# One step less between a node block's first products and its feed-forward part, in a fused GNN layer on one core

## The chip, the core and the metric

The kernel is one program on one core of one Trainium2 chip. Five engines run side by side, each through its own list of instructions in order: TensorE (PE, with its weight loads as PEld), VectorE (DVE), ScalarE (ACT), GpSimd (POOL) and SyncE (SP), which issues DMA transfers. They meet only at semaphores. The metric is the device time of one execution in microseconds (us).

## What is computed

The reference is a layer of a graph network on 50000 nodes and 25000 edges, width 128, hidden width 512, all in float32. Cut to what matters:

```python
h = jnp.maximum(_layernorm(x, axis=-1), 0.0)
xn = layernorm(h, g1, b1)
msg = jax.nn.relu(xn[src] + edge_attr)
aggr = jax.ops.segment_sum(msg, dst, num_segments=N)
t = (1.0 + eps_gin) * xn + aggr
t = jax.nn.relu(t @ Wg1 + bg1) @ Wg2 + bg2
x2 = h + t
xn2 = layernorm(x2, g2, b2)
f = jax.nn.gelu(xn2 @ Wf1 + bf1, approximate=False) @ Wf2 + bf2
return x + x2 + f
```

The edges are sorted by `dst`.

## The kernel before

Nodes go through in 98 blocks of 512 rows (the last has 336), edges in 49 chunks of 512, both from the end of the array to its start. Everything is one software pipeline. Each engine has a function `step(node, edge, halves, apart)`, and `edges_beside_nodes` calls it for t = 0, 1, 2, ... up to the number of blocks plus a lag. In step t, `node(o)` is block t - o, so one step holds up to eight different blocks, each at its own stage, and the code of `step` is the order in which that engine does them. Nothing else sets the order: there is no scheduler.

One chunk of edges takes two steps. `halves` is (0,) in odd steps and (1,) in even ones. The words odd step and even step are used in this sense from here on.

The stages of a block b, with the step in which each stands before the change:

- t = b: statistics of x (`n_stat`), relu of the normed x (`n_relu`), its statistics, and `n_var` (`variance_of`, the last VectorE operation on the block in the step). GpSimd then raises variances to the power -1/2 (`n_rstd`) in step b+1. This one instruction (`power`) takes several blocks' variances together: those of block t-1, those of a block three further on for the second norm, and in odd steps those of an edge chunk.
- t = b+1, b+2: `n_zg`, `n_in` (normed node plus the sum of its edges, `n_aggr`, which SyncE loads from memory), transposed by TensorE (`p_in`) and copied by ScalarE (`n_inT`).
- t = b+3: the product with Wg1 (`p_g`), its relu on ScalarE (`n_gT`, function `hidden`), the product with Wg2 (`p_gout`). ScalarE first puts the scaled relu into the same PSUM tile (`seed_gout`, operations named `p_gout<-n_relu,n_rstd`).
- t = b+4: VectorE adds the bias and gets x2 (`n_x2`), its statistics and variance (`s_var2`), GpSimd its power, ScalarE the normed `n_z2`, late in its step.
- t = b+5: TensorE transposes it (`p_z2`), ScalarE copies the high part (`n_z2T_high`), VectorE subtracts and gets `n_z2T_low`.
- t = b+6: the first feed-forward product (`p_f`, four column groups k, three matmuls each, at the start of TensorE's step), four gelus on ScalarE (`n_act`), the second product (`p_out`, 16 matmuls in the program, 32 passes in the trace). VectorE has put x + x2 into `p_out` in the same step (semaphore `s_x2b`).
- t = b+7: VectorE adds the last bias (`n_out`). SyncE stores it in step b+9.

In the rows of the trace the tiles `n_x2` and `n_z2` are printed as `n_x` and `n_z`, and `p_z2` as `p_z`, because trailing numbers are left out.

The edges: GpSimd gathers rows of x (`e_x`), VectorE and ScalarE norm them and add the attributes, ScalarE makes the message (`e_msg`, odd steps), TensorE sums rows of equal destination (`p_merged`, last in its odd step), and ScalarE copies the result to `e_merged` (function `merged_rows`) in the next even step. GpSimd adds these rows into memory with four scatters per chunk (`aggr_sums<-e_merged,e_index`). Two follow `power` in the even step, and wait for `s_emerged`. Two follow `power` in the odd step. Two gathers follow the scatters in every step. So GpSimd's list is, step after step: power, scatter, scatter, gather, gather. The wait for the merged rows stands ahead of the two scatters of an even step:

```python
pool.wait_ge(s_emerged, c.at + 1)
pool.wait_ge(s_eindex, c.at + 1)
```

and ScalarE's `n_z2` waits for the power of its own step:

```python
act.wait_ge(s_nrstd, b.at + 4)
```

## Time and profile before

| | |
|---|---|
| Median of 3 runs | 1058.03 us (1057.13 to 1058.07) |
| Profiled execution, its own time | 1055.18 us |
| Its span, first to last instruction | 1053.4 us |
| TensorE busy | 987.0 us (94%) |
| VectorE busy | 975.7 us (93%) |
| ScalarE busy | 855.4 us (81%) |
| GpSimd busy | 814.8 us (77%) |
| Mean granted clock of TensorE | 0.985 of full speed |

The span is the part that the profile can see; the time of the execution is 1.8 us longer. A busy share says how long an engine had an instruction under way. It doesn't say that the engine could not go faster: matmuls overlap and their ends are modelled, and spans on GpSimd are rough. So the rows on which the argument rests are mostly of the timeline, where the distance between the starts of two instructions is the real cost of the first.

### The profile page before, as it was taken

The page shows a single profiled execution, that of the slowest core. Times are in us where ns is not written, and L with a number is a line of the kernel's source. Part 1 is how long each engine was busy: PE and PEld are TensorE (multiplying, and loading weights), DVE is VectorE, ACT ScalarE, POOL GpSimd, SP SyncE. Part 2 cuts the span into 40 slices and gives each one's busy share as a digit, 9 for nine tenths or more (in the row PEclk, how much of TensorE's full clock was granted, in tenths as well). Part 3 has the DMA queues.
Part 4 walks back from the last instruction along what each step waited for, and adds up shares of the span by engine and source line. Part 5 has one row for each costly group of instructions (what it writes and reads, how often), then busy time and mean ns, then how long its engine had stood idle before and what let it go on. Part 6 is the DMA issues. An engine that isn't in the chain of part 4 may idle for free. (4 is left out here: it accounts for less than half of the span.)

```text
span 1053.4 us, 23086 instructions
## 1 busy us (share of the span) xinstructions
PE 987.0 (94%) x6684; PEld 848.8 (81%) x6684; DVE 975.7 (93%) x3499; ACT 855.4 (81%) x2158; POOL 814.8 (77%) x510
## 2 busy tenths in 40 slices
PE   1459999999999999999999999999999999999998
PEld 0347888888888888888888888888888888888877
DVE  5789999999999999999999999999999999998742
ACT  1258888988988888888888889889889888887863
POOL 6788888888888878888888888888888888875620
PEclk9779999999999999999999999999999999999999
DMA  8765766788785654554554555555555455443221
GB/s 267 203 174 129 215 171 174 230 237 236 241 246 153 154 135 114 144 143 116 138 138 126 136 142 126 125 147 131 119 149 135 112 154 130 103 120 86 58 61 40
DMA packets 110468, 156.87 MB, mean 149 GB/s; under 512 B 24835, under 2 KB 50607, under 8 KB 110334
## 3 DMA queue, kind: packets, MB, share of 16 engines
q1 hardware_dynamic: 70358, 128.99, 38.0%
q0 software_dynamic: 37760, 25.66, 17.7%
q8 instruction: 56, 0.92, 0.4%
q10 hardware_dynamic: 2216, 0.66, 0.3%
q14 instruction: 78, 0.64, 0.2%
HBM read 90.61 MB, written 64.61 MB: 147 GB/s over the span
## 5 line engine op out<-in xcount | busy, mean ns | idle before, releaser
L447 POOL DMA_INDIRECT aggr_sums<-e_merged,e_index x196 | 325.7, 1662 | 59.4 <-issue 51.6
L920 PE MATMUL p_out<-wf,n_act 128*128 128x128 f32 x3136 | 366.2, 275 | 0.0
L920 PEld LDWEIGHTS p_out<-wf,n_act 128*128 128x128 f32 x3136 | 358.0, 192 | 0.0
L456 POOL TENSOR_TENSOR n_rstd<-n_var,minus_half 128x16 f32<-128x16 f32 (+3 forms) x102 | 257.7, 2537 | 90.2 <-DVE n_var L819 36.8
L522 ACT ACTIVATE n_act<-p_f,bf1e_col 128x512 f32<-128x512 f32 x392 | 255.9, 679 | 31.1 <-PE p_f L883 26.1
L436 POOL DMA_INDIRECT e_x<-in_x,e_cols x196 | 226.4, 1155 | 60.2 <-issue 59.1
L883 PE MATMUL p_f<-n_z2T_high,wf_low 128*128 128x512 f32 x392 | 208.6, 532 | 11.1 <-ACT n_act L522 8.5
L883 PE MATMUL p_f<-n_z2T_high,wf_high 128*128 128x512 f32 x392 | 155.2, 396 | 0.0
L883 PE MATMUL p_f<-n_z2T_low,wf_high 128*128 128x512 f32 x392 | 154.6, 394 | 0.0
L604 ACT ACTIVATE n_inT<-p_in 128x512 f32<-128x512 f32 x98 | 58.5, 596 | 109.6 <-PE p_in L927 106.9
L675 DVE BATCH_NORM_STATS2 n_stat<-n_x 128x6 f32<-128x256 f32 x392 | 139.9, 418 | 0.1
L536 ACT ACTIVATE p_gout<-n_relu,n_rstd 128x128 f32<-128x128 f32 x392 | 129.3, 367 | 4.9 <-DVE n_x L802 4.5
L883 PEld LDWEIGHTS p_f<-n_z2T_high,wf_low 128*128 128x128 f32 x392 | 74.1, 189 | 71.9 <-ACT n_act L522 56.0
L572 ACT ACTIVATE n_relu<-n_x,n_minus 128x128 f32<-128x128 f32 x392 | 124.7, 396 | 8.8 <-DVE n_minus L813 8.8
L598 ACT ACTIVATE n_z<-n_x,n_rstd 128x128 f32<-128x128 f32 x392 | 125.7, 408 | 2.8 <-POOL n_rstd L456 2.8
L848 DVE SCALAR_TENSOR_TENSOR n_in<-n_zg,n_rstd,n_aggr 128x128 f32<-128x128 f32 x392 | 111.1, 346 | 10.5 <-DMA n_aggr<-aggr_sums 10.2
L912 PE MATMUL p_gout<-wg,n_gT 128*128 128x128 f32 (+1 forms) x784 | 110.6, 285 | 9.3 <-ACT p_gout L536 9.3
L837 DVE SCALAR_TENSOR_TENSOR n_zg<-n_relu,n_stat,g1e_row 128x128 f32<-128x128 f32 x392 | 111.1, 346 | 0.0
L912 PEld LDWEIGHTS p_gout<-wg,n_gT 128*128 128x128 f32 (+1 forms) x784 | 96.4, 193 | 14.4 <-ACT n_gT L530 11.9
L897 PE MATMUL p_g<-n_inT,wg 128*128 128x512 f32 x196 | 101.3, 598 | 1.4 <-ACT n_inT L604 1.4
L938 PE MATMUL p_merged<-e_msg,e_match 128*128 128x128 f32 (+1 forms) x588 | 77.0, 283 | 21.3 <-ACT e_msg L581 16.2
L883 PEld LDWEIGHTS p_f<-n_z2T_low,wf_high 128*128 128x128 f32 x392 | 74.7, 191 | 27.1 <-issue 22.5
(85 smaller groups left out, 1463.5 us busy)
## 6 DMA issues: line engine op xcount, KB each, us to landing
n_x<-in_x SPq DMA_DIRECT2D x97, 256.0 KB
n_aggr<-aggr_sums SPq DMA_DIRECT2D x97, 256.0 KB, 2.7
out_dram<-n_out SPq DMA_DIRECT2D x97, 256.0 KB
aggr_sums<-zeros SPq DMA_DIRECT2D x26, 512.0 KB, 5.2
e_dst<-in_dst_rows SPq DMA_DIRECT2D x49, 256.0 KB
e_attr<-in_attr SPq DMA_DIRECT2D x48, 256.0 KB
aggr_sums<-zeros SPq DMA_DIRECT2D x12, 1024.0 KB
e_x<-in_x,e_cols POOLq DMA_INDIRECT x196
```

The costliest lines, as they stand in the source:

```text
L436: nc.gpsimd.indirect_dma_start(out=e_x[0:r, s, j, :], out_offset=None, in_=x, in_offset=bass.IndirectOffsetOnAxis(ap=e_cols[0:r, s, 0, j:j ...
L447: nc.gpsimd.indirect_dma_start(out=aggr, out_offset=bass.IndirectOffsetOnAxis(ap=e_index[0:r, s, j:j + 1], axis=0), in_=e_merged[0:r, s, j ...
L456: return nc.gpsimd.tensor_tensor(n_rstd[0:r, s, lo:hi], n_var[0:r, s, lo:hi], minus_half[0:r, 0:(hi - lo) * J].rearrange("p (a j) -> p a j ...
L522: nc.scalar.activation(n_act[:, k, :, 0:b.rows], p_f[k % 2][:, :, 0:b.rows], ACT.Gelu, bias=bf1e_col[:, k:k + 1]).then_inc(s_act, 1)
L536: last = nc.scalar.activation(p_gout[0:r, j, :], n_relu[0:r, b.slot(4), j, :], ACT.Identity, scale=n_rstd[0:r, b.slot(8), 0, j:j + 1])
L572: last = nc.scalar.activation(n_relu[0:r, b.slot(4), j, :], n_x[0:r, b.slot(8), j, :], ACT.Relu, bias=n_minus[0:r, b.slot(8), j:j + 1])
L598: last = nc.scalar.activation(n_z2[0:r, b.slot(2), j, :], n_x2[0:r, b.slot(4), j, :], ACT.Identity, scale=n_rstd[0:r, after_three(b), 2, j ...
L675: last = nc.vector.bn_stats(to[0:rows, j:j + 2, :].rearrange("p j k -> p (j k)"), of[0:rows, j:j + 2, :].rearrange("p j d -> p d j"))
L837: last = nc.vector.scalar_tensor_tensor(n_zg[0:r, b.slot(2), j, :], n_relu[0:r, b.slot(4), j, :], n_stat[0:r, s, 1, j, 1:2], g1e_row[0:r], ...
L883: last = nc.tensor.matmul(p_f[k % 2][:, :, 0:b.rows], weights[:, k * P:(k + 1) * P], z2T[:, b.slot(2), :, 0:b.rows], start=(i == 0), stop= ...
L912: last = nc.tensor.matmul(p_gout[0:b.rows, j, :], n_gT[:, b.slot(2), j, 0:b.rows], wg2[:], start=False, stop=True, skip_group_check=True)
L920: last = nc.tensor.matmul(p_out[0:b.rows, j, :], n_act[:, k, j, 0:b.rows], wf2[:, k, :], start=False, stop=(k == KF - 1), skip_group_check ...
```

## The change

Every node stage from x2 on moves. On VectorE, x2, its statistics and its variance go from the head of step b+4 into the middle of step b+3 (`second_norm`, `second_stats`, `second_variance`), right behind the product that they read. The power of the second norm is then still taken in step b+4, but its input is there one step's end earlier. On ScalarE, `n_z2` goes from the end of step b+4 to its middle, between the third and the fourth gelu of another block, and the copy `n_z2T_high` follows in the same step. TensorE's transposes `p_z2` stand in step b+4 too, and the second product is cut in pieces around them. The feed-forward part stands in step b+5, `n_out` in step b+6, the store in b+8. There is one step less in all (`NODE_LAG` 7 to 6).

With this the order inside the steps changes. On VectorE `n_out` is first in the step and the statistics of x stand between it and x + x2. The relu's statistics and `n_z2T_low` stand later. On ScalarE `merged_rows` comes behind `hidden` and `e_msg` behind `n_z2T_high`. GpSimd's and SyncE's code is as it was, but for the lag of the stores. No instruction is added or taken away in any step.

```diff
 EDGE_LAG = 3
-NODE_LAG = 7
-SP_LAG = 9
+NODE_LAG = 6
+SP_LAG = 8
...
-                if (b := node(6)) is not None:
+                if (b := node(5)) is not None:
                     gelu(b, 0)
...
+                if (b := node(5)) is not None:
+                    gelu(b, 1)
+                if (b := node(3)) is not None:
+                    seed_gout(b, (2, 3))
+                    hidden(b)
                 if 1 in halves and 0 not in halves:
                     merged_rows(edge(3))
-                if (b := node(6)) is not None:
-                    gelu(b, 1)
-                if (b := node(3)) is not None:
-                    hidden(b)
-                    seed_gout(b, (2, 3))
...
-                if (b := node(6)) is not None:
+                if (b := node(5)) is not None:
                     gelu(b, 2)
-                    gelu(b, 3)
-                if 0 in halves and (c := edge(3)) is not None:
...
-                if (b := node(5)) is not None:
...
                 if (b := node(4)) is not None:
                     r = b.rows
...
+                if (b := node(5)) is not None:
+                    gelu(b, 3)
+                if (b := node(0)) is not None:
...
+                if (b := node(4)) is not None:
+                    act.wait_ge(s_tz2, b.at + 1)
...
+                if 0 in halves and (c := edge(3)) is not None:
+                    act.wait_ge(s_esum, c.at + 1)
...
             def z2_low(node):
-                if (b := node(5)) is not None:
+                if (b := node(4)) is not None:
...
+            def second_norm(node):
+                if (b := node(3)) is not None:
+                    r = b.rows
+                    dve.wait_ge(s_gout, b.at + 1)
+                    reached(dve, s_z2, b.at - 3)
+                    nc.vector.tensor_tensor(n_x2[0:r, b.slot(4)], p_gout[0:r], bias_of(0, r),
+                                            ALU.add).then_inc(s_x2, 1)
+
+            def second_stats(node):
+                if (b := node(3)) is not None:
+                    dve.wait_ge(s_x2, b.at + 1)
+                    stats(n_stat2[:, b.slot(8)], n_x2[:, b.slot(4)], b.rows, s_stat2)
+
+            def second_variance(node):
+                if (b := node(3)) is not None:
+                    r = b.rows
+                    dve.wait_ge(s_stat2, b.at + 1)
+                    nc.vector.tensor_scalar(n_var[0:r, after_three(b), 2], n_stat2[0:r, b.slot(8), :, 2], 1.0 / D, EPS,
+                                            ALU.mult, ALU.add).then_inc(s_var2, 1)
...
-                relu_stats(node)
+                second_norm(node)
...
-                z2_low(node)
+                second_stats(node)
...
+                    matches(c, 0)
+                second_variance(node)
+                z2_low(node)
+                relu_stats(node)
+                if c is not None:
+                    matches(c, 1).then_inc(s_ematch, 1)
                 variance_of(node)
...
-                relu_stats(node)
+                second_norm(node)
...
+                second_stats(node)
+                if c is not None:
...
+                second_variance(node)
                 z2_low(node)
-                variance_of(node)
+                relu_stats(node)
...
+                variance_of(node)
 
             def step(node, edge, halves, apart):
-                first, third, fifth = node(0), node(2), node(4)
-                if (b := fifth) is not None:
-                    r = b.rows
-                    dve.wait_ge(s_gout, b.at + 1)
-                    reached(dve, s_z2, b.at - 3)
...
-                if (b := node(7)) is not None:
+                first, third, fourth = node(0), node(2), node(3)
+                if (b := node(6)) is not None:
                     r = b.rows
                     dve.wait_ge(s_fout, b.at + 1)
...
                     nc.vector.tensor_tensor(n_out[0:r, b.slot(2)], p_out[0:r], bias_of(1, r),
                                             ALU.add).then_inc(s_nout, 1)
-                if (b := node(6)) is not None:
+                if (b := first) is not None:
+                    dve.wait_ge(q_x[b.slot(8)], 16 * (b.uses(8) + 1))
...
+                if (b := node(5)) is not None:
                     r = b.rows
...
+                if (b := first) is not None:
+                    r, s = b.rows, b.slot(8)
+                    dve.wait_ge(s_nstat, b.at + 1)
+                    nc.vector.tensor_scalar(n_minus[0:r, s], n_stat[0:r, s, 0, :, 1], -1.0, None,
+                                            ALU.mult).then_inc(s_nminus, 1)
+                    variance0_of(node)
...
+            def second_product(b, ks):
+                for k in ks:
+                    pe.wait_ge(s_act, b.at * KF + (k + 1))
+                    for j in range(J):
+                        last = nc.tensor.matmul(p_out[0:b.rows, j, :], n_act[:, k, j, 0:b.rows], wf2[:, k, :],
+                                                start=False, stop=(k == KF - 1), skip_group_check=True)
+                if ks[-1] == KF - 1:
+                    last.then_inc(s_fout, 1)
...
-                if (b := seventh) is not None:
+                if (b := sixth) is not None:
                     first_product(b, (2, 3))
                 if (b := sixth) is not None:
-                    pe.wait_ge(s_z2, b.at + 1)
-                    reached(pe, s_z2T_low, b.at)
...
+                    pe.wait_ge(s_x2b, b.at + 1)
+                    second_product(b, (0,))
                 if (b := fourth) is not None:
...
-                if (b := seventh) is not None:
-                    pe.wait_ge(s_x2b, b.at + 1)
-                    for k in range(KF):
...
+                if (b := sixth) is not None:
+                    second_product(b, (1,))
+                if (b := fifth) is not None:
+                    pe.wait_ge(s_z2, b.at + 1)
+                    reached(pe, s_z2T_low, b.at)
+                    for j in range(J):
+                        last = nc.tensor.transpose(p_z2[:, j, 0:b.rows], n_z2[0:b.rows, b.slot(2), j, :],
+                                                   ident[0:b.rows, 0:b.rows])
+                    last.then_inc(s_tz2, 1)
+                if (b := sixth) is not None:
+                    second_product(b, (2, 3))
...
-            branch(pe, EDGE_LAG, 6, step)
+            branch(pe, EDGE_LAG, 5, step)
```

ScalarE in an even step, before. The step begins with the first gelu (`n_act<-p_f`), which follows the end of the step ahead (`n_inT`, `e_relu`).

```order
L522 ACTIVATE n_act<-p_f,bf1e_col 128x512
L536 ACTIVATE p_gout<-n_relu,n_rstd 128x128 x2
L547 ACTIVATE e_merged<-p_merged 128x512
L522 ACTIVATE n_act<-p_f,bf1e_col 128x512
L530 ACTIVATE n_gT<-p_g,bg1e_col 128x512
L536 ACTIVATE p_gout<-n_relu,n_rstd 128x128 x2
L572 ACTIVATE n_relu<-n_x,n_minus 128x128 x4
L522 ACTIVATE n_act<-p_f,bf1e_col 128x512 x2
L586 ACTIVATE n_z2T_high<-p_z 128x512
L598 ACTIVATE n_z<-n_x,n_rstd 128x128 x4
```

ScalarE in an even step, after:

```order
L522 ACTIVATE n_act<-p_f,bf1e_col 128x512
L536 ACTIVATE p_gout<-n_relu,n_rstd 128x128 x2
L522 ACTIVATE n_act<-p_f,bf1e_col 128x512
L536 ACTIVATE p_gout<-n_relu,n_rstd 128x128 x2
L530 ACTIVATE n_gT<-p_g,bg1e_col 128x512
L547 ACTIVATE e_merged<-p_merged 128x512
L522 ACTIVATE n_act<-p_f,bf1e_col 128x512
L577 ACTIVATE n_z<-n_x,n_rstd 128x128 x4
L522 ACTIVATE n_act<-p_f,bf1e_col 128x512
L587 ACTIVATE n_relu<-n_x,n_minus 128x128 x4
L593 ACTIVATE n_z2T_high<-p_z 128x512
L603 ACTIVATE n_inT<-p_in 128x512
```

Before, `e_merged` is the third entry of the step; now it is the sixth, behind the second gelu, both halves of `p_gout` and `n_gT`. `n_z` (the tile `n_z2`) goes from the end of the step to behind the third gelu.

VectorE, from the head of a step (an even one), before. `n_x<-p_gout,rows` is x2, `n_stat<-n_x` x4 the statistics of x and of x2.

```order
L802 TENSOR_TENSOR n_x<-p_gout,rows 128x512
L675 BN_STATS n_stat<-n_x 128x6 x4
L813 TENSOR_SCALAR n_minus<-n_stat 128x4
L682 TENSOR_SCALAR n_var<-n_stat 128x4
L819 TENSOR_SCALAR n_var<-n_stat 128x4
L826 TENSOR_TENSOR n_out<-p_out,rows 128x512
L832 TENSOR_TENSOR p_out<-n_x 128x512
L837 SCALAR_TENSOR_TENSOR n_zg<-n_relu,n_stat,g1e_row 128x128 x4
L848 SCALAR_TENSOR_TENSOR n_in<-n_zg,n_rstd,n_aggr 128x128 x4
L675 BN_STATS e_stat<-e_relu 128x6 x2
L675 BN_STATS n_stat<-n_relu 128x6 x2
```

VectorE at the same place of an even step, after:

```order
L836 TENSOR_TENSOR n_out<-p_out,rows 128x512
L676 BN_STATS n_stat<-n_x 128x6 x2
L845 TENSOR_TENSOR p_out<-n_x 128x512
L850 SCALAR_TENSOR_TENSOR n_zg<-n_relu,n_stat,g1e_row 128x128 x4
L857 TENSOR_SCALAR n_minus<-n_stat 128x4
L683 TENSOR_SCALAR n_var<-n_stat 128x4
L867 SCALAR_TENSOR_TENSOR n_in<-n_zg,n_rstd,n_aggr 128x128 x4
L676 BN_STATS e_stat<-e_relu 128x6 x2
L699 TENSOR_TENSOR n_x<-p_gout,rows 128x512
L788 SCALAR_TENSOR_TENSOR e_extra<-e_count,spare 128x4
L793 SCALAR_TENSOR_TENSOR n_var<-e_stat,e_var 128x4
L798 TENSOR_TENSOR e_index<-e_dstf,e_extra 128x4
```

x2 goes from the head of the step to behind the edges' first statistics, and `n_out` and `p_out<-n_x`, which were neighbours, now have two statistics instructions between them.

TensorE in an even step, from the third column group of the first product on, before. `p_z<-ident,n_z` are the transposes of `n_z2`.

```order
L883 MATMUL p_f<-n_z2T_high,wf_low 128x512
L883 MATMUL p_f<-n_z2T_low,wf_high 128x512
L883 MATMUL p_f<-n_z2T_high,wf_high 128x512
L883 MATMUL p_f<-n_z2T_high,wf_low 128x512
L883 MATMUL p_f<-n_z2T_low,wf_high 128x512
L883 MATMUL p_f<-n_z2T_high,wf_high 128x512
L905 MATMUL p_z<-ident,n_z 128x128 x4
L912 MATMUL p_gout<-wg,n_gT 128x128 x4
L920 MATMUL p_out<-wf,n_act 128x128 x16
L927 MATMUL p_in<-ident,n_in 128x128 x4
```

TensorE at the same place of an even step, after:

```order
L902 MATMUL p_f<-n_z2T_high,wf_low 128x512
L902 MATMUL p_f<-n_z2T_low,wf_high 128x512
L902 MATMUL p_f<-n_z2T_high,wf_high 128x512
L902 MATMUL p_f<-n_z2T_high,wf_low 128x512
L902 MATMUL p_f<-n_z2T_low,wf_high 128x512
L902 MATMUL p_f<-n_z2T_high,wf_high 128x512
L910 MATMUL p_out<-wf,n_act 128x128 x4
L936 MATMUL p_gout<-wg,n_gT 128x128 x4
L910 MATMUL p_out<-wf,n_act 128x128 x4
L945 MATMUL p_z<-ident,n_z 128x128 x4
L910 MATMUL p_out<-wf,n_act 128x128 x8
L954 MATMUL p_in<-ident,n_in 128x128 x4
```

The transposes `p_z` go from ahead of `p_gout` to behind it and behind half of the second product.

## Rows read from the trace of the kernel before

**Rows 1.** Windows, 500 to 600 us: busy time of each engine, granted clock, DMA.
```profile
500.00:600.00 100.00, 99.16 (x687) 85.97 (x686) 98.93 (x360) 86.94 (x221) 82.50 (x51) 1.00 0.55 133
```

**Rows 2.** Timeline of VectorE, from 501 us: start, duration, engine, line, operation.
```profile
501.76 0.68 DVE L802 TENSOR_TENSOR n_x<-p_gout,rows 128x512 f32<-128x512 f32 x1
...
503.91 0.69 DVE L826 TENSOR_TENSOR n_out<-p_out,rows 128x512 f32<-128x512 f32 x1
504.70 0.70 DVE L832 TENSOR_TENSOR p_out<-n_x 128x512 f32<-128x512 f32 x1
505.31 1.13 DVE L837 SCALAR_TENSOR_TENSOR n_zg<-n_relu,n_stat,g1e_row 128x128 f32<-128x128 f32 x4
```

**Rows 3.** Timeline of TensorE, from 501 us: one even step, one odd step.
```profile
501.50 0.48 PE L883 MATMUL p_f<-n_z2T_high,wf_low 128*128 128x512 f32 x1
...
505.67 0.60 PE L905 MATMUL p_z<-ident,n_z 128*128 128x128 f32 x4
...
510.99 0.48 PE L883 MATMUL p_f<-n_z2T_high,wf_low 128*128 128x512 f32 x1
...
514.76 0.60 PE L905 MATMUL p_z<-ident,n_z 128*128 128x128 f32 x4
515.20 1.10 PE L912 MATMUL p_gout<-wg,n_gT 128*128 128x128 f32 x8
516.14 3.74 PE L920 MATMUL p_out<-wf,n_act 128*128 128x128 f32 x32
519.71 0.60 PE L927 MATMUL p_in<-ident,n_in 128*128 128x128 f32 x4
...
521.41 0.48 PE L883 MATMUL p_f<-n_z2T_high,wf_low 128*128 128x512 f32 x1
```

**Rows 4.** Timeline of ScalarE, from 502 us, in the even step.
```profile
502.49 0.69 ACT L522 ACTIVATE n_act<-p_f,bf1e_col 128x512 f32<-128x512 f32 x1 [0.29 <-PE p_f L883]
...
503.66 0.58 ACT L547 ACTIVATE e_merged<-p_merged 128x512 f32<-128x512 f32 x1
504.14 0.68 ACT L522 ACTIVATE n_act<-p_f,bf1e_col 128x512 f32<-128x512 f32 x1
...
505.86 1.28 ACT L572 ACTIVATE n_relu<-n_x,n_minus 128x128 f32<-128x128 f32 x4
...
508.64 1.29 ACT L598 ACTIVATE n_z<-n_x,n_rstd 128x128 f32<-128x128 f32 x4
```

**Rows 5.** Timeline of GpSimd, from 504 us: even step, and start of the odd one.
```profile
504.34 2.31 POOL L456 TENSOR_TENSOR n_rstd<-n_var,minus_half 128x12 f32<-128x12 f32 x1 [0.17 <-issue]
506.85 1.65 POOL L447 DMA_INDIRECT aggr_sums<-e_merged,e_index  x1 [0.20 <-issue]
...
512.09 1.04 POOL L436 DMA_INDIRECT e_x<-in_x,e_cols  x1 [0.31 <-issue]
...
514.23 2.94 POOL L456 TENSOR_TENSOR n_rstd<-n_var,minus_half 128x16 f32<-128x16 f32 x1 [1.10 <-DMA aggr_sums<-e_merged,e_index]
```

**Rows 6.** Timeline of ScalarE at three merges.
```profile
30.90 0.57 ACT L547 ACTIVATE e_merged<-p_merged 128x512 f32<-128x512 f32 x1
...
963.74 0.58 ACT L547 ACTIVATE e_merged<-p_merged 128x512 f32<-128x512 f32 x1
...
983.53 0.58 ACT L547 ACTIVATE e_merged<-p_merged 106x512 f32<-106x512 f32 x1
```

**Rows 7.** Timeline of GpSimd: the first scatter behind each of these three merges.
```profile
32.35 1.63 POOL L447 DMA_INDIRECT aggr_sums<-e_merged,e_index  x1 [4.35 <-ACT e_merged L547]
...
965.64 1.59 POOL L447 DMA_INDIRECT aggr_sums<-e_merged,e_index  x1 [1.09 <-issue]
...
985.07 2.79 POOL L447 DMA_INDIRECT aggr_sums<-e_merged,e_index  x1 [1.31 <-ACT e_merged L547]
```

**Rows 8.** Chain that ended last, 1020 us to the end: two feed-forward steps.
```profile
1029.21 0.71 PE p_f L883 x3
...
1036.36 0.71 PE p_f L883 x3
```

87 lines of the change are left out of this document (29 added, 58 removed).

## The prediction

> **What bounds the kernel now.** I read the windows first, to see which engines are full, and then the timeline of two neighbouring steps in the middle of the run, engine by engine, by the distance between starts.
>
> In the middle TensorE is busy 99.16 of 100 us and VectorE 98.93, at the full granted clock [rows 1]. Two engines can't both set the pace by chance, so the distances must decide. An even step's first product starts at 501.50, the odd step's at 510.99 and the next even one's at 521.41 [rows 3]: a pair of steps takes 19.91 us. VectorE has no gap in those two steps but one kind: `p_out<-n_x` starts 0.79 us behind `n_out`, while an operation of the same size is followed after 0.61 [rows 2]. It overwrites what `n_out` has just read and waits for its end. So VectorE sets the 19.91, with 2 x 0.18 us of that wait in it. TensorE has a little slack in the even step: from the first product to `p_z` it needs 4.17 us there and 3.77 in the odd step [rows 3], for the same work. The 0.40 is a wait for a gelu that stands behind `e_merged` on ScalarE. GpSimd is busy 82.5% [rows 1] and idles 1.10 us ahead of the odd step's power, which waits for x2's variance [rows 5].
>
> **What the change frees.** On VectorE the two statistics instructions now hide `n_out`'s end: 19.91 - 0.36 = 19.55 us per pair. The other waits of VectorE on itself still have an operation in between: x2 and its statistics are separated by three small ones. On TensorE the 0.40 goes, since `e_merged` no longer stands ahead of the second gelu: 19.91 - 0.40 = 19.51. I cost the cutting up of the second product at nothing, since the number of matmuls is the same and each piece's gelu is done by then. Bounds of this: 0 and 0.1 us for each of the two new borders, by the 0.94 us that `p_gout` takes to the next start against 0.89 for as many passes of `p_out` (3.57 / 4) [rows 3]. So both former bounds would allow about 19.55 to 19.7.
>
> **What the change binds.** The chain that I take to decide runs through GpSimd. It is laid out from the start F of TensorE's even step.
>
> 1. First gelu: F + 0.99 (502.49 - 501.50) [rows 3, 4].
> 2. `e_merged`. Before it starts at F + 2.16. The six operations from the first gelu to `n_relu` take 3.37 us, `e_merged` 0.48 of it [rows 4], and now all the others stand ahead of it: F + 0.99 + 2.89 = F + 3.88, its end at F + 4.46.
> 3. The scatter behind it. Before, GpSimd was still at its power when `e_merged` was done (504.24 against 506.65), and the scatter came 0.20 us behind the power [rows 4, 5]. Now the power can begin at about F + 1.8 and is over at about F + 4.1: its inputs are there at the end of VectorE's step, and GpSimd is free by then (the odd step's power starts at F + 11.8, steps 5 and 6 below, and power, four transfers and gaps take some 10 us, less a period of 20). So GpSimd stands at the wait. What that costs is seen at three places where the merge came last or almost: end of `e_merged` at 31.47, 964.32 and 984.11, scatter at 32.35, 965.64 and 985.07 [rows 6, 7], or 0.88, 1.32 and 0.96 us. In the second of them another wait may have come last. I take 0.95. Bounds: 0.20, the gap where all is there beforehand, and 1.32. The scatter starts at F + 5.41.
> 4. Two scatters and two gathers, and the gap to the next power: from 506.85 to 512.09 + 1.04 + 0.17 = 513.30, so 6.45 us [rows 5]. F + 11.86.
> 5. The odd step's power, 2.94 us [rows 5]: F + 14.80.
> 6. `n_z2`, 1.29 us [rows 4], which now waits for this power and not for TensorE: F + 16.1, with a few hundredths for each of two hops.
> 7. TensorE's `p_z` can start at F + 16.16. Without that wait it would be there earlier: even step 9.1 to 9.3, then 3.77 to `p_z`'s old place, and now `p_gout` and half of `p_out` ahead (0.94 + 1.79), F + 15.7. So TensorE stands some 0.5 us, and everything behind it in its list with it.
> 8. From `p_z` to the next even step: 0.44 for itself, half of `p_out` 1.79, then 1.70 for `p_in` and the merge [rows 3], 3.93 us. Next F at F + 20.09.
>
> The loop closes: the next `e_merged` hangs on the next F. 20.09 stands against 19.91, so the pair grows by 0.18 us, in spite of what VectorE and TensorE won. The even step's `n_z2` doesn't wait: its power is over at F + 4.1 and its turn on ScalarE is at about F + 4.9. The gathers of the even step end later against VectorE, but `e_stat` has over 3 us from their end; a transfer that takes longer than that would fill VectorE's slack of 0.5 us first.
>
> The loop runs while edges are there, from about step 8 to step 96, 44 pairs: 44 x 0.18 = +7.9 us.
>
> **A page against the row.** The rows say 0.88 to 1.32 us from the end of the merge to the scatter [rows 6, 7]. The Trainium skill, "Advanced Engine Details and Errata", section Miscellaneous Facts, says that a sequencer reads a semaphore in 50 to 100 ns on this chip. Taken by itself that rule would make step 3 cost about 0.1 us and the pair would be bound by VectorE and TensorE, with the result of the second rival below. The row counts more for me, since it is the same wait in the same program; what else lies in it the page does not say.
>
> **Head and tail.** The pipeline is one step shorter. At the end that saves one step of feed-forward alone, 7.15 us (1029.21 to 1036.36) [rows 8]. Three things stand against it. The last chunk's merge starts 1.7 us later in its step (F + 3.88 against 2.16), and the last two blocks wait for its scatters. Behind that wait VectorE now takes x2 and its statistics before `n_z2T_low`, which the next TensorE step needs: two operations of about 0.65 with their waits, 1.6 us. At the head, x2, its two statistics, `n_z2T_low` and `p_out<-n_x` come in one step sooner and lengthen steps that VectorE partly bounds: four pieces of 0.6 to 0.7 [rows 2], 2.6 us. Net -1.2 us, by bounds of -7 (nothing given back) and +5 (the head at half granted clock).
>
> **Sum.** 1055.18 + 7.9 - 1.2 = 1061.9 us against the profiled execution's own time. The median of the runs shown is 2.85 us above that execution, so the forecast is 1064.7 us, 0.6% slower.
>
> **The rivals.**
>
> A. The wait for the merge decides (above): 1065 us. For it: GpSimd's list is nearly full, the merge is later by 1.72 us, and `n_z2` now sits in the middle of ScalarE's step, where TensorE needs it. Against it: the margin is only 0.18 us in 20, less than the sum of my roundings. Its own range, by +-0.15 us per pair and head and tail, is 1056 to 1073.
>
> B. The late merge costs nothing, and the kernel gets faster. The point from which it decides is step 3: below 0.77 us the loop is under 19.91, and at 0.20 it takes 19.34, so VectorE and TensorE bind at 19.55 to 19.7, say 19.6. 44 x (19.6 - 19.91) = -13.6, and -1.2: 1043 us. For it speaks that the preparation of a scatter might run under the power if that ends close to F + 4.5. Against it speak all three rows of [rows 7].
>
> C. The wait costs 1.32 us, or gathers grow. The loop takes 20.46: 44 x 0.55 = +24, 1081 us. One row of three speaks for it, and its cause there is doubtful.
>
> D. The change doesn't do what it says: gain and loss cancel, with the pair at 19.9, 1057 to 1059 us. All that is needed is a step 3 of 0.75 to 0.8, or VectorE giving back its 0.36 to a new wait for `p_gout`, which ends at about F + 5.6 and is read by x2 at about that time.
>
> **How the numbers follow.** Chances: A 0.48, B 0.27, C 0.12, D 0.13. Within 0.2% of 1058.0 (1055.9 to 1060.1, about what a measurement of this kernel can tell) lie most of D and a little of A, 0.11 in all. Slower: the rest of A, C and half of what is left of D, 0.58. Faster: B and the rest, 0.31. The range reaches down to the middle of B and up to C: 1043 to 1080 leaves out the faster half of B and the slower half of C.
>
> **What the changed profile would show.** If A is right: in the middle of the run, GpSimd idles about 1 us ahead of the first scatter of every even step, released by `e_merged` or put down to issue, and no longer ahead of the odd power; ScalarE idles ahead of `n_z` in odd steps, released by the power, and TensorE ahead of `p_z` with it; VectorE falls below 98% busy; the pair is 20.0 to 20.2 us. `p_out<-n_x` should start 0.6 us behind its predecessor in any case, and TensorE's wait for the second gelu in even steps should be gone. If B is right, the pair is 19.5 to 19.7, VectorE stays at 99% and `n_z` waits for nothing. What would make me wrong beside that: a scatter or gather that changes its length because other VectorE operations now run beside it, and a wait of VectorE for `p_gout` or for gathered rows in every pair.

## The result and the profile after

The changed kernel takes 1077.55 us (median of 4 runs, 1075.56 to 1079.81) against 1058.05, a ratio of 1.0189 with a 95% interval of 1.0174 to 1.0205: 1.9% slower. (The ratios here and below are estimates of their own; the quotient of two medians can differ from them by 0.0015.) The forecast was 0.6% slower, 1065 us. The profiled span is 1075.7 us, 22.3 more than before.

The windows of the kernel after, for the stretch of [rows 1]:

```profile
500.00:600.00 100.00, 98.31 (x672) 84.94 (x672) 97.25 (x350) 85.78 (x217) 79.65 (x50) 1.00 0.53 132
```

Neither TensorE nor VectorE is full any more. The waits of the same stretch (engine, line, what it waited for; us in total, times, longest):

```profile
POOL aggr_sums L447 <- ACT e_merged L547: 8.0, 4, 2.0
...
ACT n_z L577 <- POOL n_rstd L456: 5.2, 5, 1.2
...
PEld p_z L945 <- ACT n_z L577: 2.6, 5, 0.6
DVE n_z2T_low L690 <- ACT n_z2T_high L593: 1.8, 5, 0.4
```

Read downwards it is one chain: GpSimd waits for the merge, ScalarE for GpSimd, TensorE for ScalarE, VectorE for ScalarE. The timelines give its lengths: TensorE first, the even step's first product, then the odd step's `p_z` up to the next first product.

```profile
499.26 0.48 PE L902 MATMUL p_f<-n_z2T_high,wf_low 128*128 128x512 f32 x1
...
515.40 0.66 PE L945 MATMUL p_z<-ident,n_z 128*128 128x128 f32 x4 [0.31 <-ACT n_z L577]
515.89 1.95 PE L910 MATMUL p_out<-wf,n_act 128*128 128x128 f32 x16
517.67 0.60 PE L954 MATMUL p_in<-ident,n_in 128*128 128x128 f32 x4
518.18 1.58 PE L965 MATMUL p_merged<-e_msg,e_match 128*128 128x128 f32 x12
519.51 0.48 PE L902 MATMUL p_f<-n_z2T_high,wf_low 128*128 128x512 f32 x1
```

ScalarE in the same two steps:

```profile
500.25 0.69 ACT L522 ACTIVATE n_act<-p_f,bf1e_col 128x512 f32<-128x512 f32 x1 [0.43 <-issue]
...
503.15 0.59 ACT L547 ACTIVATE e_merged<-p_merged 128x512 f32<-128x512 f32 x1
...
514.06 1.28 ACT L577 ACTIVATE n_z<-n_x,n_rstd 128x128 f32<-128x128 f32 x4 [1.02 <-POOL n_rstd L456]
...
517.46 0.62 ACT L598 ACTIVATE e_msg<-e_sum 128x512 f32<-128x512 f32 x1
```

And GpSimd:

```profile
500.30 2.31 POOL L456 TENSOR_TENSOR n_rstd<-n_var,minus_half 128x12 f32<-128x12 f32 x1
504.61 1.65 POOL L447 DMA_INDIRECT aggr_sums<-e_merged,e_index  x1 [2.00 <-ACT e_merged L547]
...
511.09 2.94 POOL L456 TENSOR_TENSOR n_rstd<-n_var,minus_half 128x16 f32<-128x16 f32 x1
```

A pair of steps takes 519.51 - 499.26 = 20.25 us, 19.91 before.

**Where the 22.3 us are.** I compare the starts of `p_g`, once per step, in both traces. "Step n" here and below is the step that begins with the nth `p_g`.

| | us |
|---|---|
| ahead of the first `p_g` | +1.9 |
| the first four steps | +3.9 |
| the five pairs up to 201 us | +1.6 |
| steps 15 to 28, 201 to 348 us in the kernel after | +7.6 |
| the 29.5 pairs from there to 947 us | +10.5 |
| up to the step that waits for the last scatters | -0.8 |
| that step and the next | +4.7 |
| the end, one step fewer | -7.2 |

The 1.9 us at the start are not the change's: in all kernels below the first `p_g` starts between 53.1 and 56.6 us. Steps 15 to 28 hold seven pairs, worth 2.4 us by the loop, so 5.2 us there are something else.

In that stretch SyncE writes zeros to memory, 1 MB at a time. Its queue before, with the load of x ahead of each zero write:

```profile
246.15 0.33 SPq L358 DMA_DIRECT2D n_x<-in_x  x1
246.52 0.55 SPq L334 DMA_DIRECT2D aggr_sums<-zeros  x1
...
256.23 0.33 SPq L358 DMA_DIRECT2D n_x<-in_x  x1
256.60 0.55 SPq L334 DMA_DIRECT2D aggr_sums<-zeros  x1
```

and after:

```profile
232.78 0.33 SPq L368 DMA_DIRECT2D e_attr<-in_attr  x1
233.15 0.43 SPq L375 DMA_DIRECT2D out_dram<-n_out  x1
233.63 0.43 SPq L358 DMA_DIRECT2D n_x<-in_x  x1
234.10 0.55 SPq L334 DMA_DIRECT2D aggr_sums<-zeros  x1
...
240.34 0.55 SPq L334 DMA_DIRECT2D aggr_sums<-zeros  x1
...
256.05 0.55 SPq L334 DMA_DIRECT2D aggr_sums<-zeros  x1
```

Before, they are 10 us apart. After, they go out in pairs, 6.2 us apart and then 15.7. The waits of SyncE's queue from 212 to 345 us say why. Before:

```profile
SPq L390 <- DMA aggr_sums<-e_merged,e_index: 45.3, 7, 6.9
SPq L358 <- DVE p_out L832: 40.2, 13, 5.3
```

The load of x waited for `p_out<-n_x`, of a block seven back, in nearly every step (13 times), and paced the queue. With the feed-forward part one step sooner that wait is gone, and what waits now is VectorE, for gathered rows (after, the same window):

```profile
DVE e_stat L676 <- DMA e_x<-in_x,e_cols: 8.5, 6, 2.3
```

### The profile page after: what moved, and what is told of

It is laid out like the page before. It is cut to its first block, busy times and chain, and to the rows that moved or that the text cites. A ratio compares the mean times of both kernels' runs of the same rounds, so it can differ in the third digit from the quotient of the medians.

```text
span 1075.7 us, 23086 instructions
## 1 busy us (share of the span) xinstructions
PE 997.4 (93%) x6684; PEld 856.2 (80%) x6684; DVE 976.3 (91%) x3499; ACT 856.2 (80%) x2158; POOL 811.3 (75%) x510
## 4 chain that ended last, share of the span: by engine, by line
DVE 29%; POOL 21%; issue 15%; PE 14%; ACT 10%; DMA 9%; POOLq 1%; DVEq 0%; SPq 0%; ACTq 0%
POOL n_rstd L456 9%; POOL e_x L436 9%; DVE n_stat L676 6%; DMA e_x<-in_x,e_cols 5%; PE p_out L910 5%; PE p_f L902 4%; DVE n_in L867 3%; ACT n_z L577 3%; DVE e_zg L806 3%; DMA aggr_sums<-e_merged,e_index 3%; POOL aggr_sums L447 3%; DVE e_stat L676 2%; DVE n_zg L850 2%; DVE n_z2T_low L690 2%; ACT n_relu L587 2%
## 5 line engine op out<-in xcount | busy, mean ns | idle before, releaser
L910 PE MATMUL p_out<-wf,n_act 128*128 128x128 f32 x3136 | 398.8, 275 | 0.0
L910 PEld LDWEIGHTS p_out<-wf,n_act 128*128 128x128 f32 x3136 | 376.4, 191 | 14.8 <-DVE p_out L845 10.7
L522 ACT ACTIVATE n_act<-p_f,bf1e_col 128x512 f32<-128x512 f32 x392 | 266.6, 680 | 53.4 <-PE p_f L902 33.9
L456 POOL TENSOR_TENSOR n_rstd<-n_var,minus_half 128x16 f32<-128x16 f32 (+3 forms) x102 | 262.8, 2588 | 39.9 <-DVE n_var L711 23.9
L436 POOL DMA_INDIRECT e_x<-in_x,e_cols x196 | 221.7, 1131 | 60.3 <-issue 57.4
L902 PE MATMUL p_f<-n_z2T_high,wf_low 128*128 128x512 f32 x392 | 203.4, 519 | 8.8 <-DVE n_z2T_low L690 6.3
L676 DVE BATCH_NORM_STATS2 n_stat<-n_x 128x6 f32<-128x256 f32 x392 | 148.4, 420 | 0.3
L587 ACT ACTIVATE n_relu<-n_x,n_minus 128x128 f32<-128x128 f32 x392 | 124.9, 397 | 11.5 <-DVE n_minus L857 11.5
L936 PE MATMUL p_gout<-wg,n_gT 128*128 128x128 f32 (+1 forms) x784 | 104.7, 277 | 4.1 <-ACT n_gT L530 4.1
L965 PE MATMUL p_merged<-e_msg,e_match 128*128 128x128 f32 (+1 forms) x588 | 80.2, 288 | 23.0 <-ACT e_msg L598 17.7
```

Of the source, the lines that this page charges most:

```text
L436: nc.gpsimd.indirect_dma_start(out=e_x[0:r, s, j, :], out_offset=None, in_=x, in_offset=bass.IndirectOffsetOnAxis(ap=e_cols[0:r, s, 0, j:j ...
L456: return nc.gpsimd.tensor_tensor(n_rstd[0:r, s, lo:hi], n_var[0:r, s, lo:hi], minus_half[0:r, 0:(hi - lo) * J].rearrange("p (a j) -> p a j ...
L522: nc.scalar.activation(n_act[:, k, :, 0:b.rows], p_f[k % 2][:, :, 0:b.rows], ACT.Gelu, bias=bf1e_col[:, k:k + 1]).then_inc(s_act, 1)
L587: last = nc.scalar.activation(n_relu[0:r, b.slot(4), j, :], n_x[0:r, b.slot(8), j, :], ACT.Relu, bias=n_minus[0:r, b.slot(8), j:j + 1])
L676: last = nc.vector.bn_stats(to[0:rows, j:j + 2, :].rearrange("p j k -> p (j k)"), of[0:rows, j:j + 2, :].rearrange("p j d -> p d j"))
L902: last = nc.tensor.matmul(p_f[k % 2][:, :, 0:b.rows], weights[:, k * P:(k + 1) * P], z2T[:, b.slot(2), :, 0:b.rows], start=(i == 0), stop= ...
```

## The experiments

All ratios are to the kernel before, with their 95% intervals. The pair is taken between the 34th and the 50th `p_g` of the profile, in the quiet part of the run, where no zeros are written: it is the mean of eight pairs of one profiled execution. Each kernel has only one. The theory T is the prediction's: the late merge holds up GpSimd, and the loop over GpSimd, ScalarE and TensorE sets the pace. The rivals were that something else in the new order costs (VectorE's new waits, the cut-up second product, the transfers).

**The merge's place, three kernels.** The changed kernel, with only `merged_rows` moved: ahead of the second gelu as before the change (e1), behind the second gelu (e2), behind the third (e3). The edit of e2; in e1 the two lines stand behind `seed_gout(b, (0, 1))`, in e3 behind `gelu(b, 2)`:

```diff
                 if (b := node(5)) is not None:
                     gelu(b, 1)
+                if 1 in halves and 0 not in halves:
+                    merged_rows(edge(3))
                 if (b := node(3)) is not None:
                     seed_gout(b, (2, 3))
                     hidden(b)
-                if 1 in halves and 0 not in halves:
-                    merged_rows(edge(3))
```

> The changed kernel with one thing undone: ScalarE copies the merged rows where it did before, third in its even step (about 2.2 us behind the first product's start instead of 3.9). Theory 1, the loop through GpSimd (merge, scatter, gathers, power, n_z, p_z) decides: GpSimd no longer idles ahead of the even step's first scatter, the loop shrinks by 1.7 us from 20.25 to about 18.5 and stops to bind. Then the pair of steps is that of VectorE or TensorE, 19.6 to 19.95 (the second gelu is late again by 0.4 us), and the time 1055 to 1066 us. Theory 2, the new places of x2 and n_z2 cost by themselves (VectorE waits for p_gout, the second product for x + x2): the pair stays at 20.1 to 20.25 and the time within 3 us of 1077.

> The changed kernel with the merge copied behind the second gelu, two operations earlier than in the change. Theory 1: the merge is 1.15 us earlier, the loop is 20.25 - 1.15 = 19.1 us and binds no more, and the second gelu isn't late: 19.55 to 19.75 us a pair, 1048 to 1058 us in all. Theory 2: within 3 us of 1077.

> The changed kernel with the merge copied one operation later, behind the third gelu: a dose. Theory 1: everything in the loop moves by the gelu's 0.57 us, so the pair of steps takes 20.8 us instead of 20.25 and the whole 44 x 0.55 = 24 us more, about 1101 us. Theory 2, and any theory in which GpSimd's wait is slack: within 3 us of 1077.

| | pair | median | ratio |
|---|---|---|---|
| e1 | 19.98 | 1059.37 | 1.0019 (1.0005 to 1.0032) |
| e2 | 19.59 | 1050.58 | 0.9923 (0.9900 to 0.9946) |
| after | 20.25 | 1077.55 | 1.0189 (1.0174 to 1.0205) |
| e3 | 21.10 | 1109.42 | 1.0497 (1.0470 to 1.0525) |

The later the merge from e2 on, the longer the pair, and with the merge 1.16 us sooner than in the change (two seedings and `n_gT`), the kernel beats the one before. From e1 to e2 the pair falls by 0.4 us, as TensorE's wait for the second gelu goes. The windows of e2 show both engines full:

```profile
500.00:600.00 100.00, 100.00 (x696) 87.68 (x696) 99.73 (x365) 88.71 (x224) 84.02 (x52) 1.00 0.55 133
```

In e3 the chain's waits have grown together:

```profile
POOL aggr_sums L447 <- ACT e_merged L547: 10.3, 4, 2.6
ACT n_z L577 <- POOL n_rstd L456: 9.4, 5, 1.9
PEld p_z L945 <- ACT n_z L577: 6.8, 5, 1.4
DVE n_z2T_low L690 <- ACT n_z2T_high L593: 6.1, 5, 1.2
```

The merge in e3 stands 0.56 us later than in the kernel after (one gelu), and the pair grew by 0.85, more than the 0.55 expected. What is added is in GpSimd's power of the odd step, the same instruction on the same shape, which takes 2.94 us in the kernel after and here

```profile
522.05 3.39 POOL L456 TENSOR_TENSOR n_rstd<-n_var,minus_half 128x16 f32<-128x16 f32 x1
```

while the stretch from the first scatter to the power is 6.31 us instead of 6.48: 0.56 + 0.45 - 0.17 = 0.84. What makes the power longer isn't shown; so e3 bears out the loop, but not a dose of one to one. e1 falls back to TensorE's old wait for the gelu behind the merge: `PEld p_f <- ACT n_act` has 5.7 us in 16 waits there, 2.4 in 10 in e2.

**Gathers ahead of the scatters in GpSimd's even steps (e4).** It unhooks the gathers from the wait for the merge without touching ScalarE:

```diff
-                if 1 in halves and not 0 in halves:
-                    merged_first(edge, apart)
 ...
                 if 1 in halves and (c := edge(0)) is not None:
                     gather(c, range(PAIR, J))
+                if 1 in halves and not 0 in halves:
+                    merged_first(edge, apart)
```

> The changed kernel with GpSimd's order changed in even steps alone: the two gathers stand ahead of the two scatters, so that they fill the wait for the merge. Theory 1: the wait of 2.0 us ahead of the first scatter is gone, the odd step's power is ready about 1 us or more sooner, ScalarE's n_z waits no more, the pair is 19.55 to 19.8 us and the time 1050 to 1062. Theory 2: within 3 us of 1077.

The pair is 19.60: with the merge as late as in the change (F + 3.88 in both), the loop is broken. The total is 1069.59, ratio 1.0098 (1.0071 to 1.0126), because steps 15 to 29 take 169.6 us, against 158.1 after and 150.3 before. Its page of waits for 300 to 345 us says what the later scatters cost there:

```profile
DVE n_in L867 <- DMA n_aggr<-aggr_sums: 7.3, 2, 4.2
POOL aggr_sums L447 <- DMA aggr_sums<-e_merged,e_index: 7.3, 2, 3.9
```

**The same edit in the kernel before (e5).** There `merged_rows` is moved behind `hidden` and the second seeding.

> The kernel before, with the odd-numbered half of ScalarE's steps changed in one point: e_merged stands behind hidden and the second half of the seeding, one gelu and two seedings later than before. In the kernel before, GpSimd is at its power when e_merged ends (504.24 against 506.65), so 2 us of delay should be hidden under the power. Theory 1 (a late merge costs only where GpSimd stands at the wait): the pair of steps keeps 19.91 us or falls by at most 0.1, since TensorE's wait of 0.40 behind e_merged goes but VectorE still needs 19.91; total 1054 to 1060 us. Rival 2 (the later merge is itself what costs in the changed kernel, wherever GpSimd stands, for example by later transfers against VectorE): the pair is 20.1 us or more, total above 1066 us.

1059.58 us, ratio 1.0019 (1.0008 to 1.0030), pair 19.91. A merge 1.7 us later costs nothing in the loop as long as GpSimd is still at its power when it is done: the even step's scatter starts 0.20 us behind the power, at 506.71. So lateness is no price in the loop by itself. In the tail it is one: the step that waits for the last scatters takes 15.6 us in e5 and 11.8 in the kernel before.

**VectorE's gain alone, in the kernel before (e6), and with the merge of e2 (e7).** e6 puts `n_out` ahead of the statistics of x:

```diff
+                if (b := node(7)) is not None:
+                    ...
+                    nc.vector.tensor_tensor(n_out[0:r, b.slot(2)], p_out[0:r], bias_of(1, r),
+                                            ALU.add).then_inc(s_nout, 1)
                 if (b := first) is not None:
                     dve.wait_ge(q_x[b.slot(8)], 16 * (b.uses(8) + 1))
```

> The kernel before, with one instruction of VectorE moved: n_out stands ahead of the two statistics of x, so that p_out<-n_x no longer follows it directly. Theory 1 (VectorE's wait for the end of n_out, 2 x 0.18 us, is what VectorE has to give back, and TensorE stands close behind): VectorE needs 19.55 us for a pair and TensorE with its gelu wait about 19.8, so the pair takes 19.7 to 19.85 and the kernel 1049 to 1056 us. If TensorE isn't bound by that gelu wait at all, the pair is 19.55 and the total 1042 us. Rival 2 (the 0.18 us is no wait for n_out's end, or n_out now waits for TensorE's p_out): the pair stays at 19.91 or grows, total 1058 us or more.

> The kernel before, with both single edits: n_out ahead of the two statistics of x on VectorE, and e_merged behind the second gelu in odd edge halves on ScalarE. Nothing else of the change is in it: the feed-forward part stays seven steps behind. Theory 1 (the two gains of the change come from these two places alone, and its losses from the late merge and from head, transfers and tail of the shortened pipeline): the pair is 19.55 to 19.6 us, as in the changed kernel with the merge behind the second gelu, and head and tail are those of before, so the total is 1040 to 1046 us, the fastest so far. Rival 2 (the gains need x2 and z2 in the middle of the step): the pair stays at 19.8 or more and the total at 1053 us or more.

Both missed: 1083.18 us, 1.0246 (1.0217 to 1.0275), and 1081.73 us, 1.0228 (1.0200 to 1.0256), with pairs of 20.46 and 20.45. `p_out<-n_x` no longer waits, but something else has taken over. In e6 SyncE and VectorE show:

```profile
515.21 0.33 SPq L390 DMA_DIRECT2D n_aggr<-aggr_sums  x1
```

```profile
518.21 1.14 DVE L848 SCALAR_TENSOR_TENSOR n_in<-n_zg,n_rstd,n_aggr 128x128 f32<-128x128 f32 x4 [0.85 <-DMA n_aggr<-aggr_sums]
```

`n_out` ahead of the statistics makes x2's variance 0.60 us later, and GpSimd's power of the odd step, which waited 1.10 us for it before [rows 5], waits 1.37. Its scatters land later, SyncE issues `n_aggr` at once behind them, and VectorE's `n_in` now waits for it. In the kernel before 3.53 us lie between that issue (502.84) and `n_in` (506.37); in e6 it is 3.00 us, and the load itself takes 2.8. The odd step's power is also longer in both kernels, 3.26 us for the 2.94 of before. I read this loop from its waits and have not closed its sum, so its cause is argued, not shown. What the two runs do show: with x2 and its variance left in their old place, moving `n_out` alone doesn't bring VectorE's 0.36 us.

**SyncE's queue (e8).** The changed kernel with one number:

```diff
-                before, = counts(b, b.at - 7)
+                before, = counts(b, b.at - 6)
```

> The changed kernel, with one number of SyncE's step changed: the load of x waits until p_out<-n_x is done for one block more (it waited for the block that frees its slot of 8). In the kernel before, this load waited for VectorE in each step and so spaced the zero writes of 1 MB at 9.8 and 10.1 us; in the changed kernel it never waits and they go out in pairs, 6.2 and 14.2 us apart, right ahead of the gathers of even steps, and VectorE waits for gathered rows, 8.5 us in 212 to 345 us. Theory 1 (these bursts cause the loss in that stretch): the zero writes are 10 us apart again, VectorE's waits for e_x go, the stretch between the 15th and the 29th step is 3 to 6 us shorter, the pair in the middle stays at 20.25, and the total is 1071 to 1075 us. Rival 2 (the gathers themselves start too late and the bursts don't matter): total within 1 us of the changed kernel's 1077.6.

1071.52 us, 1.0137 (1.0113 to 1.0162), 6.0 us less than the changed kernel. Steps 15 to 29 take 152.8 us (158.1 after), exactly eight long and seven short steps of the quiet part (8 x 11.03 + 7 x 9.22), the waits for `e_x` are gone, and the pair is still 20.24. The zero writes go out at 232.23, 242.39 and 252.47. So the lost pacing is the 5 us. It isn't that a zero write goes out close to other transfers: in e8 as well `e_attr`, `n_out`, x, zeros and `n_aggr` are issued within 2.13 us, from 250.99 to 253.12. Whether the distance between zero writes counts, or their place ahead of the gathers, no run tells apart.

**Together (e9), with edits at the tail (e10), the head (e11), both (e12).** e9 is e2 with e8's number. e10 adds that the last chunk's merge stands one gelu sooner, and that VectorE takes `n_z2T_low` ahead of x2 once no block enters. e11 adds to e9, for block 0 only, a power of its own ahead of the gathers of the step before (in two more places, left out here, the joint power skips this block and ScalarE's `n_z2` waits for the new one):

```diff
+                if (nb := node(3)) is not None and nb.is_number(0):
+                    pool.wait_ge(s_var2, 1)
+                    power(nb.rows, after_three(nb), 2, 3).then_inc(s_rstd2, 1)
                 if 0 in halves and (c := edge(0)) is not None:
                     gather(c, range(0, PAIR))
```

> The changed kernel with both single edits that helped it: e_merged behind the second gelu, and SyncE's load of x waiting for p_out<-n_x of one block more. Theory 1 (the two losses lie in different places and add): the pair stays at 19.57 us in the middle, and the stretch from the 14th to the 29th step falls from 152.8 us to 147 to 148; with 1050.6 us for the merge edit alone the total is 1043 to 1046 us. Rival 2 (the pacing only repairs what the late merge causes, so with the merge early it brings nothing): 1050 us.

> As e9, with two edits that act only at the end: the last chunk's e_merged stands in its former place, one gelu sooner, and once no new block enters, VectorE takes n_z2T_low ahead of x2 and its statistics. Theory 1 (these are the two terms of 1.7 and 1.6 us that I said the tail gives back; behind the second gelu the first is only 1.0): the step that waits for the last scatters falls from 15.5 to 13 us and the total by 2 to 3 us against e9. Rival 2 (the tail is set by GpSimd's scatters and transfers alone): within 0.8 us of e9.

> As e9, with one edit that acts only at the head: GpSimd takes the power for x2 of block 0 by itself ahead of the gathers of the step before, instead of behind them with the power of the next block, so that n_z2 of block 0 need not wait. In the changed kernel ScalarE waited 5.13 us for it at 73.45, and n_relu, p_z, p_in and p_g stood behind. Theory 1 (this queue is why the head lost 5.8 us where I said 2.6): the step that took 16.5 us, and 10.07 before, falls by 2.5 to 4 us, and the total by 2 to 4 us against e9. Rival 2 (the head is set by n_aggr's scatters and by feed-forward work at half clock): within 1 us of e9.

> As e9, with the edits of e10 and of e11 together. If both add: 4 to 7 us under e9, 1037 to 1042 us, 1.5 to 2% faster than the kernel before. If neither works: the 1043 to 1046 us of e9.

| | pair | steps 15 to 29 | last-scatter step | median | ratio |
|---|---|---|---|---|---|
| e2 | 19.59 | 152.8 | 15.5 | 1050.58 | 0.9923 |
| e9 | 19.89 | 149.8 | 15.4 | 1053.97 | 0.9964 (0.9952 to 0.9975) |
| e10 | 19.87 | 149.9 | 13.3 | 1048.30 | 0.9906 (0.9883 to 0.9929) |
| e11 | 19.90 | 149.8 | 14.9 | 1053.80 | 0.9961 (0.9948 to 0.9974) |
| e12 | 19.86 | 149.9 | 11.5 | 1049.34 | 0.9922 (0.9895 to 0.9948) |

e9 missed: the stretch got 3.0 us shorter, not the 5 to 6 expected, and the pair 0.3 longer. In e10 the step that waits for the last scatters is 2.1 us shorter, as expected. The median of e10 is 5.7 us under that of e9, more than the edits can explain, while the two profiled executions take the same (1052.3 and 1052.2), with e10's first `p_g` 1.9 us later. e11 gained nothing. ScalarE's wait did go:

```profile
68.70 1.28 ACT L584 ACTIVATE n_z<-n_x,n_rstd 128x128 f32<-128x128 f32 x4 [0.16 <-POOL n_rstd L456]
```

where the kernel after has

```profile
73.45 1.27 ACT L577 ACTIVATE n_z<-n_x,n_rstd 128x128 f32<-128x128 f32 x4 [5.13 <-POOL n_rstd L456]
```

but in e11 the first product waits for VectorE instead, whose `n_z2T_low` stands behind a late `n_in` and x2:

```profile
76.30 0.79 PE L909 MATMUL p_f<-n_z2T_high,wf_low 128*128 128x512 f32 x1 [2.87 <-DVE n_z2T_low L697]
```

**Is it the pacing that makes the pair 19.9? (e13, e14.)** e13 is e10 without the pacing; e14 paces only the first 34 blocks, while zeros are written.

> The changed kernel with e_merged behind the second gelu and the two edits of the tail, without the pacing of SyncE's load. Theory 1 (the pacing gains 3 us while zeros are written and loses 8 us behind that stretch, where the pair was 19.86 us with it and 19.57 without): the pair is 19.57 in the middle, the stretch of the 14th to the 29th step 152.8 us, and the total 1044 to 1047 us, 2 to 5 us under e10. Rival 2 (the 19.86 came from something else, and the pair is 19.86 here too): 1050 to 1053 us.

> As e13, with SyncE's load paced only for the first 34 blocks, that is only while zeros are written. Theory 1: both gains are kept, the stretch of the 14th to the 29th step is 149.8 us and the pair behind it 19.57 us, so the total is 1041 to 1044 us, 3 us under e13. Rival 2 (the pace that the pair has once taken stays, with or without the wait): the pair stays at 19.86 behind the stretch and the total is 1048 to 1050 us, as e10.

e13: 1054.21 us, 0.9955 (0.9940 to 0.9970), pair 19.86, steps 15 to 29 153.7. e14: 1049.97 us, 0.9936 (0.9916 to 0.9957), pair 19.87, steps 15 to 29 150.2. So it is not the pacing: e13 has the code of e2 in the middle and yet the other pace. Two patterns exist for the same instructions. In the slower one TensorE waits longer for gelus behind the merge. Weight loads in e2, then in e13, 500 to 600 us:

```profile
PEld p_f L902 <- ACT n_act L522: 2.4, 10, 0.2
```

```profile
PEld p_f L913 <- ACT n_act L522: 4.3, 13, 0.4
```

The traces show where the patterns part. It is one hop, the first gelu of the even step behind the first product. In e2, and in the same way in nearly every pair of the quiet part in the kernels before and after and in e1 to e8:

```profile
526.47 0.47 PE L902 MATMUL p_f<-n_z2T_high,wf_low 128*128 128x512 f32 x1
527.45 0.69 ACT L522 ACTIVATE n_act<-p_f,bf1e_col 128x512 f32<-128x512 f32 x1 [0.27 <-PE p_f L902]
```

and in e13, and in the same way in e9 to e14:

```profile
529.99 0.48 PE L913 MATMUL p_f<-n_z2T_high,wf_low 128*128 128x512 f32 x1
531.22 0.69 ACT L522 ACTIVATE n_act<-p_f,bf1e_col 128x512 f32<-128x512 f32 x1 [0.53 <-PE p_f L913]
```

The gelu starts 0.98 us behind the product in e2 and 1.23 to 1.29 in e9 to e14, `e_merged` is late by as much (2.72 and 3.00 us behind the product), and so is TensorE's step (9.20 and 9.48 us from the even to the odd step's first product). ScalarE is idle before that gelu in both, and `e_relu` ahead of it ends 0.70 us behind the product in both. Why the gelu then starts later, and what decides which pattern an execution settles in, stays open. In the stretch with the zeros the pacing brings the same 3 to 4 us in e14 against e13 as in e9 against e2.

## Why the prediction was right in its mechanism and wrong in its size

**The loop.** The change made the loop of steps 1 to 8 the bound, as rival A had it. Each step against the rows of after, counted from F = 499.26:

| step | forecast | measured |
|---|---|---|
| 1, first gelu | F + 0.99 | F + 0.99 |
| 2, `e_merged` | F + 3.88 | F + 3.89 |
| 3, from its end to the scatter | 0.95 | 0.87 |
| 4, to the odd power | 6.45 | 6.48 |
| 5, the power | 2.94 | 2.94 |
| 6, `n_z2` to `p_z` | 1.29 and some hundredths | 1.37 |
| 7, `p_z` | F + 16.16 | F + 16.14 |
| 8, `p_z` to the next F | 3.93 | 4.11 |

The step that was mis-sized is step 8, by 0.18 us. `p_z` itself, `p_in` and the merge take 0.49, 0.51 and 1.33 us to the next start, where [rows 3] have 0.44 for `p_z` and 1.70 for the last two together. Step 8 counted only TensorE's own work behind `p_z`. But TensorE's merge, `p_merged`, reads `e_msg`, and that stands in ScalarE's list behind the delayed `n_z`: gelu, `n_relu`, `n_z2T_high` and then `e_msg`, which the change put there and which ends at 518.08 (row above). The weight loads of the kernel after:

```profile
517.57 0.47 PEld L954 LDWEIGHTS p_in<-ident,n_in 128*128 128x128 f32 x4
518.15 1.42 PEld L965 LDWEIGHTS p_merged<-e_msg,e_match 128*128 128x128 f32 x12
```

and of e1, where `e_msg` is done 0.19 us before the first load of `p_merged`:

```profile
506.46 0.47 PEld L954 LDWEIGHTS p_in<-ident,n_in 128*128 128x128 f32 x4
506.90 1.42 PEld L965 LDWEIGHTS p_merged<-e_msg,e_match 128*128 128x128 f32 x12
```

The first weight load of `p_merged` starts 0.07 us behind the end of `e_msg` and 0.59 behind the load of `p_in` in the kernel after, in e3 and in e8, the three whose loop binds, and 0.44 behind it in all others. So 0.15 us of the 0.18 are a wait for `e_msg`, too short for the lists of waits to show. In e1, e2, e4 and e9 to e14 `p_z` to the next first product is 3.92 us, which is the forecast's 3.93. As the whole growth of 0.18 per pair was the difference of two sums near 20, this term nearly doubled it; 0.08 less in step 3 and some hundredths more in steps 2, 4 and 6 leave 0.34. The three quiet stretches of the table (1.6 and 10.5 us, and 2.4 inside steps 15 to 28) make 14.5 us, forecast 7.9.

**Step 3.** From the end of `e_merged` to the scatter it is 0.87 us here, next to the low end of 0.88 to 1.32 that [rows 6, 7] gave. I called this what it costs to stand at the wait. e1 says otherwise: there GpSimd's power ends 0.56 us after `e_merged`, and the scatter still starts 0.88 us behind `e_merged`:

```profile
511.87 1.82 POOL L447 DMA_INDIRECT aggr_sums<-e_merged,e_index  x1 [0.32 <-issue]
```

`e_merged` ends at 510.99 and the power at 511.55 in that trace. In the quiet part of all kernels but e4 the scatter starts, in nearly every pair, at the later of two moments, 0.87 us behind the end of `e_merged` or 0.20 behind the power's. The Trainium skill, "Advanced Engine Details and Errata", section Miscellaneous Facts, gives 50 to 100 ns for reading a semaphore; no run here shows a blocked scatter start that fast. The idle time was longer than I said (2.00 us against about 1) since the even power ended sooner (F + 3.35 for F + 4.1), without effect.

**What the change frees.** Right: e2 and e4, with the loop broken in two different ways, run at 19.59 and 19.60, and I had 19.55 to 19.7 for both former bounds together. TensorE's 0.40 is there too: the pair falls from 19.98 in e1 to 19.57 in e2, if the one disturbed pair of its eight is left out. But 19.86 is possible with the same code, and in e6 and e7 VectorE's part of the gain did not come by itself.

**Rivals.** B, the late merge costs nothing, fell with the loop. C priced the wait at 1.32 and would have given 20.46; its total of 1081 was nearer than mine by luck, since the wait is 0.87. D fell with the measured pair.

**Head and tail, net -1.2.** Measured 3.9 - 0.8 + 4.7 - 7.2 = +0.6, without the start. The tail's terms hold: -7.2 against -7.15, and the merge's later place cost 1.7 us (last-scatter step 14.5 in e1, 16.2 after). The head cost 3.9 instead of 2.6. The wait of `n_z2` for GpSimd looked like its cause and isn't (e11); with it gone VectorE's list holds up the same product. The clock isn't it either: from 53 to 97 us it is 0.77 of full speed in the kernel after and 0.83 in the one before, but in e5 it is 0.74, and its first four steps take 40.3 us like those of the kernel before. What else the head's 1.3 us are stays open.

**The stretch with the zero writes, 5 us, was in no term.** I costed moved engine work and GpSimd's queue but not SyncE's. The diff shows `SP_LAG` change and leaves `load_x` alone; that the same wait then falls due one step sooner, and stops being one, had to be read from SyncE's waits. e8 shows it.

Sum of the misses: 6.6 (loop), 5.2 (zero writes), 1.3 (head), 0.5 (tail), 1.9 (start of the profiled run) make 15.5, and 22.3 less the 6.7 forecast is 15.6. Against the median, 1077.55, the forecast of 1064.7 missed by 12.9 only, because it carried 2.85 us for a profiled execution faster than the median, and that of the kernel after (1077.4) lies at its median.

## What to carry to other kernels

When work is pulled ahead in a software pipeline, follow each instruction that it pushes back until the loop closes, across the in-order lists of all engines, and with it everything that stands behind it in its list: here TensorE waited not only for the late `n_z` but also for the `e_msg` four places behind it; here an `e_merged` 1.7 us later made a pair 20.25 us instead of 19.98 in one pipeline (after and e1) and cost nothing in the other (e5). If the loop's sum and the present bound differ by 0.2 us in 20, the error of each term counts as often as the loop turns: 0.15 us here weighed nearly as much as the 0.18 forecast. Look also at waits that vanish: a wait that never ends last on an engine's path may be what spaces the transfers.

## What the runs showed of the hardware

The first of the two scatters on GpSimd starts 0.87 us behind the end of the ScalarE instruction that writes its rows, whether GpSimd stands at the wait before that end (by 1.12 us in the kernel after, by 1.69 in e3) or comes to it 0.56 us after it (e1). When the power before the scatter ends later still, the scatter follows the power by 0.20 us (0.69 us after the merge in e5, 2.41 in the kernel before). In the tail the last pair, released by a transfer, starts 1.21 us after it, as the profile's chain reads it:

```profile
1014.60 7.08 DMA aggr_sums<-e_merged,e_index
...
1021.73 1.21 issue
1022.94 2.76 POOL aggr_sums L447
```

The same power on GpSimd (128x16) takes 2.94 us in the quiet part of most kernels, 3.26 in e6 and e7 and 3.39 in e3. Zero writes of 1 MB issued 6.2 and 15.7 us apart went with waits of up to 2.3 us for gathered rows; issued 10 us apart, in the same steps and with the same transfers beside them, with none (e8). And in the quiet part the same instructions ran at 19.59 us per pair in one execution (e2) and at 19.86 in another (e13), apart by the start of one gelu.
